# State-update matmuls issued before the output matmuls in each chunk of a retention scan

## The reference

```python
def step(S, qkv):
    qb, kb, vb = qkv
    attn = jnp.einsum('bhid,bhjd->bhij', qb, kb) * D[None]
    o_intra = jnp.einsum('bhij,bhjd->bhid', attn, vb)
    o_inter = jnp.einsum('bhid,bhde->bhie', qb * cross_q, S)
    S_new = gC * S + jnp.einsum('bhjd,bhje->bhde', kb * cross_k, vb)
    return (S_new, o_intra + o_inter)
```

## Time and profile before

| | us |
|---|---|
| median of 9 runs | 2856.68 (2845.64 to 3088.14) |
| the profiled execution | 2845.64 |
| its span on the slowest core (core 1) | 2844.1 |
| PE busy | 2308.3 (81%) |
| DVE / ACT / POOL busy | 830.2 / 764.6 / 443.0 |
| the eight scans, by windows that hold them | 513.1 |

### The profile page before, as it was taken

The page is one execution under the profiler, slowest core; times in us unless marked ns, Lnnn a source line. Parts: engine busy times, 40 slices in busy tenths (PEclk is TensorE's granted clock), DMA queues, the critical chain, the costliest instruction groups (busy, mean ns, idle before and its releaser), DMA issues. The chain is left out here.

```text
span 2844.1 us, 32662 instructions; the slowest of 8 cores (2831.4 to 2844.1 us)
## 1 busy us (share of the span) xinstructions
PE 2308.3 (81%) x10736; PEld 1033.2 (36%) x10736; DVE 830.2 (29%) x1989; ACT 764.6 (27%) x1532; POOL 443.0 (16%) x564
## 2 busy tenths in 40 slices
PE   1597969697379999999916879796963999999998
PEld 0243424243134444444413334342421444444444
DVE  3524243333232112211244252423332321121112
ACT  2434353434101111111134443434340111111111
POOL 2012030302300220121020211203023002201210
PEclk9797989797689999999957989797975999999999
DMA  9211030200773774675380202002009637746743
GB/s 199 48 21 40 1 60 1 53 8 18 135 145 103 75 75 97 110 72 56 119 185 30 34 27 30 31 2 59 1 23 158 139 91 75 73 107 100 74 55 116
DMA packets 296914, 202.16 MB, mean 71 GB/s; under 512 B 212144, under 2 KB 261424, under 8 KB 296624
## 3 DMA queue, kind: packets, MB, share of 16 engines
q0 software_dynamic: 234240, 96.50, 29.2%
q1 hardware_dynamic: 62512, 103.59, 11.7%
HBM read 254.45 MB, written 41.94 MB: 104 GB/s over the span
## 5 line engine op out<-in xcount | busy, mean ns | idle before, releaser
L936 PE MATMUL P<-xnT,wgu 128*128 128x512 bf16 x1536 | 351.8, 382 | 24.4 <-DMA wgu<-fuw 15.8
L947 PE MATMUL P<-xnT,wgu 128*128 128x512 bf16 x1536 | 347.2, 379 | 0.0
L963 PE MATMUL P<-wd_sb,hT 128*128 128x512 bf16 x1536 | 332.2, 379 | 6.7 <-DVE hT L992 6.7
L992 DVE TENSOR_TENSOR hT<-sg_sc,P 128x1024 bf16<-128x1024 bf16 x96 | 117.3, 1222 | 594.9 <-PE P L947 594.9
L842 PE MATMUL P<-wo_sb,ogl 128*128 128x512 bf16 x1024 | 240.1, 395 | 43.8 <-DVE ogl L863 39.4
L975 ACT ACTIVATE sg_sc<-P 128x1024 bf16<-128x1024 f32 x96 | 98.3, 1024 | 561.5 <-PE P L936 561.4
L630 DVE SCALAR_TENSOR_TENSOR S<-S,U_ps 128x512 bf16<-128x512 bf16 x240 | 154.3, 684 | 285.4 <-PE U_ps L601 285.4
L913 POOL DMA_DIRECT2D wgu<-fgw x92 | 80.4, 874 | 982.6 <-PE P L947 982.6
L936 PEld LDWEIGHTS P<-xnT,wgu 128*128 128x128 bf16 x1536 | 147.2, 98 | 221.1 <-issue 58.1
L401 POOL TENSOR_TENSOR og_sb<-o_win,ggb 128x512 bf16<-128x512 bf16 x128 | 148.0, 1165 | 491.3 <-ACT o_win L673 491.3
L466 PE MATMUL U_ps<-wv_sb,xnT 128*128 128x512 bf16 x1024 | 222.3, 379 | 0.0
(11 more groups left out here) (94 smaller groups left out, 2241.9 us busy)
## 6 DMA issues: line engine op xcount, KB each, us to landing
wgu<-fgw POOLq DMA_DIRECT2D x96, 256.0 KB, 4.7
wgu<-fuw POOLq DMA_DIRECT2D x96, 256.0 KB, 5.3
ln_x<-x SPq DMA_DIRECT2D x32, 512.0 KB, 9.5
og_spill<-og_st SPq DMA_DIRECT2D x128, 128.0 KB, 1.7
ogl<-og_spill SPq DMA_DIRECT2D x128, 128.0 KB, 2.6
xc_sb<-x SPq DMA_DIRECT2D x32, 512.0 KB, 4.5
out<-o_sb SPq DMA_DIRECT2D x32, 512.0 KB, 5.7
wd_sb<-fdw POOLq DMA_DIRECT2D x48, 256.0 KB, 40.7
```

The source lines that it names most:

```text
L936: ins = te.matmul(fgps[:, n * 512:(n + 1) * 512], wgu[:, par * 1024 + k * 128: par * 1024 + (k + 1) * 128], G.xnT[:, k * T + tok0 + n * 51 ...
L947: ins = te.matmul(fups[:, n * 512:(n + 1) * 512], wgu[:, 2048 + par * 1024 + k * 128: 2048 + par * 1024 + (k + 1) * 128], G.xnT[:, k * T + ...
L963: ins = te.matmul(ps[:, n * 512:(n + 1) * 512], hT[:, k * 1024 + mc * 128:k * 1024 + (mc + 1) * 128], wd_sb[:, k * D + n * 512:k * D + (n ...
L992: ins = v.tensor_mul(out=hT[:, m * 1024:(m + 1) * 1024], in0=sg_sc[:, (m % 2) * 1024:(m % 2 + 1) * 1024], in1=fups[:, :])
```

## The change

The block of the two U matmuls, with its waits, is moved from behind the block of the o matmuls to ahead of it. In the changed kernel the U matmuls are L587, and the o matmuls are L596 and L602. No instruction is added or taken away, no semaphore value changes, and the streams of DVE, ACT, POOL and SP are the same.

```diff
                     if c >= LAG:
                         og_tr(c - LAG)
+                    WG(te, sKT.h, b["kt"] + c + 1)
+                    for d in range(2):
+                        WG(te, sS.h, b["st"] + 2 * c + d - 1)
+                        ins = te.matmul(U_ps[:, d * 512:(d + 1) * 512],
...
+                        sTu.inc(ins)
                     WG(te, sAT.h, b["at"] + c + 1)
                     WG(te, sOE.h, b["oe"] + 2 * c - 2)
                     WG(te, sS.h, b["st"] + 2 * c)
...
                     sTo.inc(ins)
-                    WG(te, sKT.h, b["kt"] + c + 1)
-                    for d in range(2):
-                        WG(te, sS.h, b["st"] + 2 * c + d - 1)
-                        ins = te.matmul(U_ps[:, d * 512:(d + 1) * 512],
...
-                        sTu.inc(ins)
                     if c + 2 < NCH:
                         at_kt(c + 2)
```

More of the change, by code:

```diff
@@ L583, in _ @@
                         og_tr(c - LAG)
+                    WG(te, sKT.h, b["kt"] + c + 1)
+                    for d in range(2):
+                        WG(te, sS.h, b["st"] + 2 * c + d - 1)
+                        ins = te.matmul(U_ps[:, d * 512:(d + 1) * 512],
+                                        ktok[:, par * 256 + d * 128:
+                                             par * 256 + (d + 1) * 128],
+                                        vtb[:, c * 512:(c + 1) * 512],
+                                        start=True, stop=True)
+                        sTu.inc(ins)
                     WG(te, sAT.h, b["at"] + c + 1)
```

## The result

The changed kernel takes 2958.4 us (median of all 10 runs, 2952.0 at best) against 2856.0 before (median of all 32, 2845.6 at best). The ratio is 1.0357, 95% interval 1.0344 to 1.0371, which is 102 us. The forecast was 2960 us. In some runs of both kernels the cores of a die were granted a lower clock and the time was over 1.5% above that kernel's best (up to 3207 us before and 3297 after); ratios here leave those out.

A forecast was written before the change was run, and what follows sets the result against it. A PE-ACT loop through ktok and the o matmuls was taken to bound the scans. U's 93 us plus 15 for other work, less 2, made 106; on 2845.6 that is 2952, taken as 2960 to compare medians; range 2925 to 3005.

The forecast's parts named there:

- The loop: In the scans PE and ACT wait for each other; U inside adds 0.43 us a turn at full clock, 0.85 at half.
- U's own time: The two U matmuls' issue time in the scan turns, 93 us with 0.70 of them at half clock.
- The clock's effect on the rest: More scan turns at half clock slow the other work: 15 us, less about 2 for each head's first three turns.
- Waits and room: In the scans, U's ktok and state waits add almost nothing (0.4 us, dropped); the S update already had room, counted zero.
- The first: Rival: the clock stays low through the scans, 151 us more, 3008 us; chance 0.12.
- the second: Rival: the scans' share of half clock does not change, 85 us more, 2942 us; chance 0.17.
- The third: Rival: U goes into PE's idle time ahead of the key transposes, no change, 2857 us; chance 0.03.
- The fourth: Rival: o really waits for the state, so U ahead is faster by 119 us, 2738 us; chance 0.02.

The follow-up runs named there:

- fill runs: Matmuls into an unused PSUM bank between scores and key transposes, against the kernel before: four with U ahead of o 1.0067; three in the order before 0.9927.
- the one with early ktok: Against the kernel before: ACT makes ktok of chunk c+1 ahead of its o_ps copy, two banks, og_tr last; U behind o 0.9503, U ahead 0.9317.
- the fastest kernel: Against the kernel before: ktok of chunk c+1 made ahead of the o_ps copy, two banks, og_tr last, U ahead of o; 0.9317, median 2655 us.

## Why the prediction was right

- **The loop.** Right. The step was that og_tr, o and ACT's work up to ktok make a loop, and that U adds its issue time to it. The turns are 4.08 and 5.31 us (4.16 and 5.30 forecast), the waits 237.4 and 344.8 us (240 to 250, and 350). Moving U to another place outside the loop cost nothing, and half of U cost a bit over half.
- **U's own time, 93 us of the 106.** Too high, for two reasons. First, the price at full clock: a turn grew by 4.08 - 3.73 = 0.35 us and not by 0.43. The lines show where: U to o takes 0.46 (387.21 to 387.67), but U starts 0.23 us after og_tr (386.98 to 387.21), where o started 0.34 after it (226.05 to 226.39). At half clock the turn grew by 0.86, as forecast. Second, the share: I had U at half clock in 0.70 of the cases, for a mean near 560 ns; its mean of 510 ns gives (510 - 380) / 253 = 0.51. Together, an estimate: 128 x (0.51 x 0.86 + 0.49 x 0.35) = 78 us.
- **The clock's effect on the rest, 13 us.** Too low. By the same reckoning the share of half clock went from 0.45 to 0.75 for the two o matmuls with S (494 to 569 ns) and from 0.43 to 0.60 for the first one (488 to 531): 240 x 0.30 x 0.212 + 128 x 0.17 x 0.212 = 20 us, and perhaps 3 for the transposes. 78 + 23 = 101, beside 102 measured. That the forecast came within 4 us of it is in part luck: U was about 15 us too high and the rest 10 too low. What failed is the assumption that one share holds for the whole turn. In the changed order U follows the idle time and o stands last, and 246 of 299 falls of the clock come within the o matmuls.
- **The same assumption in the fill runs.** I expected 50 us from full clock in the order before and got 26 in the scans' 120 turns (458.6 to 432.4). 0.54 is the share of the U matmuls of the slowest core; the turns themselves, 0.72 us apart, are on average only (3.82 - 3.60) / 0.72 = 0.30 of the way to half clock.
- **Waits and room.** Right. In the changed kernel PE was idle 0.6 us in all ahead of U and not at all ahead of o, and the clock of the scans, 0.69, lies in the 0.60 to 0.70 of the forecast.
- **Rivals.** The first (clock low throughout) and the second (share unchanged) stand on either side of what happened: the clock in the scans fell from 0.77 to 0.69, neither to half nor not at all. For U alone the second came true (0.54 before, 0.51 after); it failed on o. The third (PE's idle time takes U in) is refuted by the result and by the two runs with U outside and half outside of the loop. The fourth, that the state is what o waits for, is false for this kernel and true for the one with early ktok, where 104 us of PE's idle time end with DVE's S and the changed order gains 2.0%. Its mechanism was right, and its point of decision is where I had put it: when the update ends last.
- **Small slips.** 0.54 of 256 is 138 and not 140, worth half a us. And the end of the o matmuls lies 0.15 us ahead of ACT's copy (226.60 + 0.59 to 227.34); the 0.3 us count from the end of their issue. No sum rests on it.

On the clock, the section "A second HAM failure mode: psum-queue depth-cycling" of "TensorE: Matmul & The Clock Gate" in the Trainium skill names short idle times between groups of matmuls as a cause of swings. The runs agree and give a size: 53.8 of 98.7 us here, and a granted clock of 0.98 in the scans once fill matmuls shorten the idle time.

## What to carry to other kernels

Before moving a piece of work on an engine, find the loop that sets the turn and ask on which side of its waits the piece stands: outside it is free, inside it costs its issue time in every turn. The same order lost 3.6% while ACT's output work closed the loop and gained 2.0% once that loop was opened and the state's update closed it, so such a choice must be taken again after each change of the bound. Where PE's clock swings, idle time has a second price, here as large as the first.

## What the runs showed of the hardware

Useless matmuls made a kernel faster: 336 of them in PE's idle time took the granted clock in the scans from 0.77 to 0.98 and the kernel from 1 to 0.9927 (interval 0.9893 to 0.9960).

Three of the profiled executions (half of U ahead, U after the scores, and the fastest kernel) also hold a value between the two levels, 0.8125, in the clock records of the four cores of one die, for 40 to 241 us of each; those of the kernel before and of the changed one do not. On the slowest core of the kernel with half of U ahead (core 4) it lies in the last stage. Windows, columns as in the earlier trace rows:

```profile
2500.00:2690.00 190.00, 182.89 (x822) 81.78 (x837) 36.95 (x31) 23.82 (x23) 24.52 (x28) 0.99 0.60 95
2700.00:2890.00 190.00, 187.10 (x703) 77.84 (x717) 28.11 (x23) 20.49 (x20) 26.26 (x30) 0.81 0.52 65
```

In the first window, before it sets in, the clock is 0.99, in the second 0.81 throughout, with fewer matmuls (703 against 822) in the same time (in the kernel before, that stage is at 1.00 from 2700 us on, with 618 in 140 us); this core's span was 2949.3 us where the other cores had 2893 to 2928. In the fastest kernel's turn above, where the record is at 0.8125 too, the 128x512 matmuls start 0.26 us apart (226.87 to 227.38 for two), between the 0.22 and 0.43 of the two levels. "TensorE: Matmul & The Clock Gate" of the Trainium skill, in the caveats of its section "Seeing it yourself", gives 13/16, which is this value, as the clock of a whole die once three of its cores run dense matmuls. Here all eight cores ran the same dense stages in every execution, and it came in three profiled ones out of eleven after the kernel before, so by these runs it is not the rule; what set it off stays open. Ratios of a few tenths of a per cent should be read with that in mind, which is why the verdicts above rest on the scans too.
